# A two-layer graph convolution with experts behind it: 21 dense units ahead of the first gathered group in place of 63, kept out of the first row buffer

## The chip, the cores and the metric

The kernel runs on one core of a Trainium2 chip. The metric is the device time of one execution in microseconds (us); the time before is the median of three executions. The engines are named as the profile names them: PE (TensorE) multiplies matrices, PEld is its weight load, DVE (VectorE), ACT (ScalarE) and POOL (GpSimd) compute elementwise, POOL also issues the indirect DMAs, and SP (SyncE) issues the plain ones; SPq is its queue.

## The reference, cut to what matters

```
x: (6250, 256); src, dst, edge_weight: 100000 edges, sorted by dst
def gcn_conv(x, src, dst, w, W, b, n):
    xw = x @ W
    deg = segment_sum(w, dst)
    dinv = where(deg > 0, rsqrt(deg), 0)
    norm = dinv[src] * w * dinv[dst]
    return segment_sum(xw[src] * norm[:, None], dst) + b
out = relu(gcn_conv(layernorm(x), W1, b1))        # every node also has an edge to itself
out = gcn_conv(out, W2, b2)
x = x + relu(batchnorm(out) * gamma + beta + layernorm(x))
x = x + moe_ffn(layernorm(x))                     # 8 experts, the best two of each row, gelu
```

What the change touches is `segment_sum(xw[src] * norm)` of the first convolution: for each destination node, the weighted sum of its sources' rows. The kernel sums the rows first and multiplies by W behind that.

## The kernel before, in words

The nodes are 49 tiles of 128 (`NT`). The kernel works in three stages: it prepares the graph, it runs the two convolutions (`layer` 0 and 1 in the code; the change's words call them layer 1 and 2), and it runs batch norm, gate and experts.

**Two ways for an edge's row.** The sorted edges are 56 groups of 14 x 128. The last 40 groups (`GG`) are *gathered*: POOL issues 14 indirect DMAs a group (L575), each bringing 128 rows into the row buffer `G`; DVE builds a matrix with the edges' weights for each (`build`, L1122, into `S`); PE multiplies the two (L1554). `G` and `S` have two halves, so the gathers of group k+2 wait until the products of group k are done (`summed`). The first 16 groups are *dense*: in four blocks of four, each block a 6272 x 512 matrix of weights that POOL scatters into DRAM beforehand (L560, 224 indirect DMAs, 56 a block) and that is read back as 49 *units* of 128 x 512 (256 KB). A unit is two matmuls (L1508) against the tile's rows in `X`; 196 units make the dense part of a layer. When a block's 49 units are done, DVE adds the result to the sums (L1137) before PE goes on to the next block, and `FINISH` counts from there.

**Where the units stand.** The first `BEFORE[0]` units of layer 0 run *early*, ahead of the first gathered group: SP loads them seven at a time (`load_early`, L442) into three regions that are used in turn: `A_in` and the two halves of `G`. The others run inside the groups: `PER_GROUP` says that `up` units in `per` groups go between the 14 products. SP loads them one by one into the seven slots of `A_in` (`load_pairs`, L453), each as soon as the unit seven before it is done (`dense_used`, which PE counts up at a group's last unit). Since the early units lie in `G`, POOL's first two groups of gathers wait for `dense_used` (49 for the first, 56 for the second):

```
elif layer == 0:
    pool.wait_ge(dense_used, BEFORE[0] - (2 - k) * ASLOTS)
```

Between the early units PE also turns the 49 tiles (`turn_set`, L1498), four tiles at a time.

**The end of layer 0.** A tile is *finished* when its sums are complete: PE multiplies by W1 (`linear`, L1467), DVE adds the bias (L1059), ACT takes relu (L711), PE turns the result again (L1456) and DVE copies it (L1049); SP stores seven tiles at a time for the next layer's gathers (L466). In layer 0 a tile is finished only after the last dense unit, at most four tiles in a group, in the order of the tiles; the rest follow behind the last group (`linear_rest`, `finish_rest`). With 63 early units and five a group, the units end in group 26: groups 27 to 39 finish 46 tiles (eleven times four, then one and one, since the last tiles' edges lie in the last groups), and three are left. Layer 1's gathers (the same L575) wait for all stores.

**What sets the order.** Each engine runs its program in the order in which the code writes it; semaphores tie them together. POOL's queue in order: 224 scatters, 560 gathers of layer 0, 560 of layer 1, then its work for the experts.

Of the kernel before, what the change touches and what calls it, by code (L numbers as in the profile page):

```python
# [12 lines left out]
P = 128  # L13
CH = 7
GT = 14
# [9 lines left out]
ASLOTS = 7  # L25
# [31 lines left out]
def gnn_ffn(nc, x, src, dst, edge_weight, g_W1, g_b1, g_W2, g_b2, g_gamma, g_beta,  # L57
            gate_w, gate_b, e_W1, e_b1, e_W2, e_b2, out):
    N, D = x.shape
# [23 lines left out]
    BW = BG * P  # L83
# [15 lines left out]
    with ExitStack() as ctx:  # L99
# [17 lines left out]
        G = arena[:, 0:at]  # L117
        S = arena[:, at:at + 2 * GT * P]
# [3 lines left out]
        assert 11 * RW <= 2 * GT * P  # L122
        at += 2 * GT * P
        A_in = arena[:, at:at + ASLOTS * BW]
        early_at = [A_in] + [G[:, h * GT * D:(h + 1) * GT * D] for h in range(2)]
        assert GT * D == ASLOTS * BW
        rows_at = at + ASLOTS * BW
        src_h, dst_h, w_h, key_h = [arena[:, rows_at + n * RH:rows_at + (n + 1) * RH] for n in range(4)]
        src_h, dst_h = src_h.bitcast(I32), dst_h.bitcast(I32)
# [160 lines left out]

        LOADS = 9
        ROW_LOADS = 8
        BEFORE = (63, 0)
        assert BEFORE[0] % ASLOTS == 0 and NT % ASLOTS == 0 and (UNITS - BEFORE[0]) % ASLOTS == 0
        SETS = -(-NT // 4)
        PER_GROUP = ((5, 1), (16, 3))
        TURN_LAG = 3

        def region(q):
            return (q - BEFORE[0] // ASLOTS + 1) % 3  # L300

        def units_of(layer):
            
# [84 lines left out]
        with nc.Block() as block:  # L388
# [3 lines left out]
            def _(sp):  # L392
# [42 lines left out]
                def load_early():  # L435
                    for q in range(BEFORE[0] // ASLOTS):
                        n = q * ASLOTS
                        if n % NT == 0:
                            sp.wait_ge(paired[n // NT], 16 * BG * GT)
                        if q >= 3:  # L440
                            sp.wait_ge(dense_used, (q - 2) * ASLOTS)
                        sp.dma_start(early_at[region(q)].rearrange("p (u c) -> p u c", c=BW),  # L442
                                     pairs[n * P * BW:(n + ASLOTS) * P * BW, :].rearrange("(u p c) o -> p u (c o)", p=P, c=BW)
                                     ).then_inc(early_in[region(q)], 16)

                def load_pairs(layer):
                    for n in range(BEFORE[layer], UNITS):
# [69 lines left out]
            def _(pool):  # L517
# [46 lines left out]
                for layer in range(2):  # L564
                    for n in range(2):
                        pool.wait_ge(y_stored[n], 16 * SLOT_CH[n] * (layer + 1))
                    with pool.If(general == 0):
                        for k in range(GG):
                            if k >= 2:
                                pool.wait_ge(summed, GG * layer + k - 1)  # L570
                            elif layer == 0:
                                pool.wait_ge(dense_used, BEFORE[0] - (2 - k) * ASLOTS)
                            for j in range(GT):
                                n, t = k % 2 * GT + j, (DG + k) * GT + j
                                pool.indirect_dma_start(  # L575
                                    G[:, n * D:(n + 1) * D], None, y_tab[layer],
                                    bass.IndirectOffsetOnAxis(srcT[:, t:t + 1], 0)).then_inc(gathered[n // 2], 16)
                    with pool.Else():
                        with pool.Fori(0, ET) as i:
                            pool.wait_ge(gen_staged, i + (ET * layer + 1))  # L580
                            take_turn(gen_turn, i + (ET * layer + 1))
                            pool.indirect_dma_start(
                                G[:, 0:D], None, y_tab[layer],
                                bass.IndirectOffsetOnAxis(gstg[:, 0:1], 0)).then_inc(gen_gathered, 16)
# [258 lines left out]
            def _(dve):  # L843
# [264 lines left out]
                def aggregate(layer):  # L1108
# [9 lines left out]
                    with dve.If(general == 0):  # L1118
                        def build(k):
                            for j in range(GT):  # L1120
                                n, t = k % 2 * GT + j, (DG + k) * GT + j
                                v.tensor_scalar(S[:, n * P:(n + 1) * P], iota[:, 0:P], dst_rel[:, t:t + 1],  # L1122
                                                wT[:, t:t + 1], ALU.is_equal, ALU.mult).then_inc(s_ready, 1)

                        def base_of(k):
                            return dve.value_load(base_i[0:1, k:k + 1], min_val=0, max_val=NP - P)

                        def add_block(b):
                            for k in range(BG):
                                n = DG * layer + b * BG + k  # L1130
                                at = base_of(b * BG + k)
                                if k == 0:
                                    dve.wait_ge(dense_used, UNITS * layer + (b + 1) * NT)
                                dve.wait_ge(added, GG * layer + so_far[0])
                                dve.wait_ge(dense_added, n)
                                a = acc[:, :, bass.ds(at, P)]
                                v.tensor_tensor(a, a, psum[:, 6:8, k * P:(k + 1) * P], ALU.add).then_inc(dense_added, 1)  # L1137
                            so_far[1] += BG

                        def add_group(k):  # L1140
                            at = base_of(DG + k)
                            dve.wait_ge(sum_turned, GG * layer + k + 1)
                            dve.wait_ge(added, GG * layer + k)
                            dve.wait_ge(dense_added, DG * layer + so_far[1])
                            a = acc[:, :, bass.ds(at, P)]
                            v.tensor_tensor(a, a, bank(2 * (k % 2) + 1, D).rearrange("p (c n) -> p c n", c=KC),  # L1146
                                            ALU.add).then_inc(added, 1)
                            so_far[0] += 1

                        so_far = [0, 0]  # L1150
                        blocks = 0
                        build(0)
                        for k, (first_unit, units) in enumerate(units_of(layer)):
                            while blocks < NB and (blocks + 1) * NT <= first_unit:
                                add_block(blocks)
                                blocks += 1
                            if k + 1 < GG:
                                build(k + 1)
                            while blocks < NB and (blocks + 1) * NT <= first_unit + units:
                                add_block(blocks)  # L1160
                                blocks += 1
                            if layer == 1 and k and 0 in FINISH[1][1][k - 1]:
                                set_shift(chain_fast)
                            for i in FINISH[layer][1][k]:
                                finish(layer, i)
                            add_group(k)
                        dve.wait_ge(added, GG * (layer + 1))
                        v.memset(dscr[:, :], 0.0).then_inc(agg_done, 1)
                        finish_rest(layer, NT - len(FINISH[layer][2]), chain_fast)
# [213 lines left out]
            def _(pe):  # L1383
# [104 lines left out]
                def aggregate(layer):  # L1488
# [13 lines left out]
                    with pe.If(general == 0):  # L1502
                        def unit(n, table):
                            b, t = divmod(n, NT)
                            if t == 0 and b + NB * layer:
                                pe.wait_ge(dense_added, BG * (NB * layer + b))
                            for c in range(KC):
                                ins = m.matmul(bank(6 + c, BW), X[:, t * D + c * P:t * D + (c + 1) * P], table,  # L1508
                                               start=(t == 0), stop=(t == NT - 1))
                            return ins  # L1510
# [19 lines left out]
                        if layer == 0:  # L1530
                            for n in range(3):
                                turn_set(n)
                            sets, batches = 3, BEFORE[0] // ASLOTS
                            for q in range(batches):
                                pe.wait_ge(early_in[region(q)], q // 3 * 16 + 16)
                                for u in range(ASLOTS):
                                    ins = unit(q * ASLOTS + u, early_at[region(q)][:, u * BW:(u + 1) * BW])
                                    if u == ASLOTS - 1:
                                        ins.then_inc(dense_used, ASLOTS)
                                    if u % 3 == 2 and sets < SETS:  # L1540
                                        turn_set(sets)
                                        sets += 1
                        pe.wait_ge(self_added, NT * (layer + 1))
                        used = 0
                        for k, (first_unit, units) in enumerate(units_of(layer)):
# [190 lines left out]
```

## Time and profile before

| | |
|---|---|
| time, median of 3 runs | 2427.9 us (2425.14 to 2429.19) |
| profiled execution: span from its first to its last instruction | 2758.3 us |
| busy in it: PE / POOL / DVE / ACT | 2008.3 / 1699.3 / 899.0 / 424.7 us |
| mean granted TensorE clock | 0.826 |

The profiled execution is 330.4 us longer than the median of the timed ones; its rows have to be read with that in mind. In a row of the timeline stand the start, the duration, the engine, the line, the operation, the tiles, how often, and in brackets the idle time before it and what ended that. An fp32 matmul is two rows of PE, so a dense unit is four rows and a group's 14 products are 28.

### The profile page before, as it was taken

The numbers are of one execution on the slowest core, as the hardware profiler recorded it, in microseconds if no ns is written. First come the engines' busy times: TensorE is split into PE (matmuls) and PEld (weight loads), VectorE is DVE, ScalarE is ACT, GpSimd is POOL, SyncE is SP. The second block draws the span as 40 slices with busy tenths as digits, with TensorE's granted clock in tenths as the row PEclk, the third lists the DMA queues.
The fourth block names the chain that finished last, engine by engine and source line by source line (L and its number), as shares of the span: only waits on it lengthen the run. The fifth ranks groups of instructions, "written<-read, shape, count | busy, mean of one in ns | idle before, by whom it ended". The sixth has DMA issues, their size and how long they took to land.

```text
span 2758.3 us, 29927 instructions
## 1 busy us (share of the span) xinstructions
PE 2008.3 (73%) x8514; PEld 1397.0 (51%) x8515; DVE 899.0 (33%) x2676; ACT 424.7 (15%) x1140; POOL 1699.3 (62%) x1679
## 2 busy tenths in 40 slices
PE   0353249887778886665688888888885473999998
PEld 0251014444445444554445555554554362899997
DVE  7970001111122113342113323232323776333332
ACT  1610000000000000111000000000000465344443
POOL 2887732566656666665765666755665544566665
PEclk6555559988889987878889999998998555999999
DMA  9993013454445443334444545544545313688885
GB/s 321 336 312 101 27 40 124 135 165 152 147 138 168 147 151 103 119 117 119 142 148 143 175 154 170 158 145 141 170 154 186 101 58 129 179 209 207 214 210 137
DMA packets 263529, 431.17 MB, mean 156 GB/s; under 512 B 38800, under 2 KB 147023, under 8 KB 263279
## 3 DMA queue, kind: packets, MB, share of 16 engines
q1 hardware_dynamic: 180591, 253.79, 27.8%
q0 software_dynamic: 81088, 173.80, 23.8%
q10 hardware_dynamic: 1728, 2.13, 0.2%
q8 instruction: 55, 0.90, 0.1%
q14 instruction: 67, 0.55, 0.1%
HBM read 339.36 MB, written 91.16 MB: 156 GB/s over the span
## 4 chain that ended last, share of the span: by engine, by line
another core or an unknown queue 34%; PE 28%; issue 17%; DVE 13%; DMA 3%; ACT 1%; SPq 1%; POOL 1%; DVEq 1%; POOLq 0%; ACTq 0%
PE psum L1508 8%; PE psum L1679 6%; PE psum L1687 6%; PE psum L1554 4%; DVE arena L1122 3%; DMA arena<-pair_weights 1%; DMA out_dram<-ACC 1%; PE psum L1467 1%; SPq L453 1%; PE psum L1670 1%; DVE edge_cols L1214 1%; DVE stats L1220 1%; PE psum L1526 1%; DVE ACC L926 1%
## 5 line engine op out<-in xcount | busy, mean ns | idle before, releaser
L575 POOL DMA_INDIRECT arena<-conv_rows,edge_cols x1120 | 1065.3, 951 | 694.3 <-issue 338.7
L1508 PE MATMUL psum<-arena,X 128*128 128x512 f32 x1568 | 805.7, 636 | 220.5 <-issue 141.4
L1554 PE MATMUL psum<-arena 128*128 128x256 f32 x2240 | 595.3, 399 | 78.2 <-issue 64.8
L1554 PEld LDWEIGHTS psum<-arena 128*128 128x128 f32 x2240 | 447.1, 203 | 271.1 <-issue 218.1
L1508 PEld LDWEIGHTS psum<-arena,X 128*128 128x128 f32 x1568 | 314.6, 202 | 512.8 <-issue 434.4
L1146 DVE TENSOR_TENSOR ACC<-ACC,psum 128x256 f32 x80 | 33.8, 422 | 1037.9 <-remote 441.5
L560 POOL DMA_INDIRECT pair_weights<-scale_b,mean_b x224 | 252.3, 1126 | 116.7 <-issue 67.9
L1122 DVE TENSOR_SCALAR arena<-iota,edge_cols 128x128 f32<-128x128 f32 x1120 | 298.1, 359 | 6.1 <-issue 5.9
L650 POOL DMA_INDIRECT out_dram<-ACC x105 | 166.3, 1583 | 108.9 <-DMA out_dram<-ACC 78.3
L729 ACT ACTIVATE arena<-psum 128x256 f32<-128x256 f32 x80 | 30.4, 380 | 1311.7 <-remote 727.5
L1679 PE MATMUL psum<-ACC,arena 128*128 128x128 f32 x1680 | 208.3, 277 | 0.2 <-DVE ACC L1356 0.2
L1679 PEld LDWEIGHTS psum<-ACC,arena 128*128 128x128 f32 x1680 | 199.4, 194 | 0.6 <-issue 0.6
L1687 PE MATMUL psum<-arena,ACC 128*128 x840 | 198.9, 380 | 0.2 <-ACT ACC L820 0.2
L1687 PEld LDWEIGHTS psum<-arena,ACC 128*128 128x128 f32 x840 | 151.7, 191 | 16.9 <-issue 0.6
L1526 PE MATMUL psum<-ident,arena 128*128 128x128 f32 x160 | 38.3, 326 | 155.2 <-ACT arena L729 143.1
L820 ACT ACTIVATE ACC<-psum,b1e 128x128 f32<-128x128 f32 x420 | 120.1, 369 | 108.7 <-issue 69.0
L1374 DVE TENSOR_TENSOR ACC<-psum,b2e 128x256 f32<-128x256 f32 x105 | 44.7, 425 | 252.1 <-PE psum L1687 178.1
L638 POOL DMA_INDIRECT ACC<-rows_for_experts,ACC x105 | 103.4, 985 | 35.7 <-issue 25.3
L1526 PEld LDWEIGHTS psum<-ident,arena 128*128 128x128 f32 x160 | 20.5, 156 | 203.6 <-ACT arena L729 174.9
L1114 DVE COPY ACC<-psum 128x512 f32<-128x512 f32 (+1 forms) x25 | 15.9, 675 | 227.6 <-remote 179.8
L1427 PE MATMUL psum<-ACC,arena 128*128 128x6 bf16 x784 | 56.2, 202 | 34.9 <-DVE arena L993 30.4
L721 ACT ACTIVATE ln<-ACC 128x256 f32<-128x256 f32 x49 | 20.4, 417 | 359.7 <-issue 173.9
(287 smaller groups left out, 1532.4 us busy)
## 6 DMA issues: line engine op xcount, KB each, us to landing
arena<-pair_weights SPq DMA_DIRECT2D x329, 256.0 KB
arena<-in_L_ffn_W_dram SPq DMA_DIRECT2D x113, 512.0 KB, 7.9
pair_weights<-zeros SPq DMA_DIRECT2D x4, 12544.0 KB, 44.2
arena<-conv_rows,edge_cols POOLq DMA_INDIRECT x1120
arena<-pair_weights SPq DMA_DIRECT2D x9, 1792.0 KB
conv_rows<-X SPq DMA_DIRECT2D x14, 896.0 KB
X<-in_x_dram SPq DMA_DIRECT2D x12, 896.0 KB
rows_for_experts<-ACC SPq DMA_DIRECT2D x7, 910.0 KB, 4.2
```

The source lines that it names most:

```text
L560: pool.indirect_dma_start(pairs, bass.IndirectOffsetOnAxis(cell_i[:, t:t + 1], 0), cell_w[:, t:t + 1], None).then_inc(paired[b], 16)
L575: pool.indirect_dma_start(G[:, n * D:(n + 1) * D], None, y_tab[layer], bass.IndirectOffsetOnAxis(srcT[:, t:t + 1], 0)).then_inc(gathered[n ...
L638: pool.indirect_dma_start(xs[:, u * DX:(u + 1) * DX], None, rows_x, bass.IndirectOffsetOnAxis(slot_i[:, n:n + 1], 0)).then_inc(xs_in[u // ...
L650: pool.indirect_dma_start(out, bass.IndirectOffsetOnAxis(slot_i[:, n:n + 1], 0), ys[:, u * D:(u + 1) * D], None, bounds_check=N - 1, oob_i ...
L820: ins = a.activation(hT[:, slot * H + c * P:slot * H + (c + 1) * P], psum[:, 2 + slot, c * P:(c + 1) * P], ACT.Gelu, bias=b1e[:, bass.ds(e ...
L1122: v.tensor_scalar(S[:, n * P:(n + 1) * P], iota[:, 0:P], dst_rel[:, t:t + 1], wT[:, t:t + 1], ALU.is_equal, ALU.mult).then_inc(s_ready, 1)
L1427: ins = m.matmul(bank(2 + h, 6 * DQ)[:, r * 6:(r + 1) * 6], hot[:, :, j], w_group[:, (q * GT + j) * 6:(q * GT + j + 1) * 6], start=(j == 0 ...
L1508: ins = m.matmul(bank(6 + c, BW), X[:, t * D + c * P:t * D + (c + 1) * P], table, start=(t == 0), stop=(t == NT - 1))
L1526: ins = m.transpose(bank(2 * (k % 2) + 1, D)[:, c * P:(c + 1) * P], sum_rows[:, at:at + P], ident[:, :])
L1554: ins = m.matmul(bank(2 * (k % 2), D), S[:, n * P:(n + 1) * P], G[:, n * D:(n + 1) * D], start=(j == 0), stop=(j == GT - 1))
L1679: ins = m.matmul(psum[:, 2 + s, c * P:(c + 1) * P], w1s[:, s4 * KC * H + k * H + c * P:s4 * KC * H + k * H + (c + 1) * P], xsT[:, s * D + ...
L1687: ins = m.matmul(bank(4 + s, D), hT[:, s * H + c * P:s * H + (c + 1) * P], w2e[:, bass.ds(e * (HC * D) + c * D, D)], start=(c == 0), stop= ...
```

## The change

It takes 21 early units in place of 63. They are three loads, each with a region of its own: the second half of `G`, `A_in`, and the buffer `S` of DVE's matrices. So the first half of `G` is free from the start: the first group of gathers waits for no unit, the second for seven. DVE builds its first matrices only after all 21 are done, since `S` holds units until then. The other 175 units of layer 0 go six to a group. PE turns a set of tiles after every second early unit, not every third, and the sets that are left behind the last.

```
-        early_at = [A_in] + [G[:, h * GT * D:(h + 1) * GT * D] for h in range(2)]
-        assert GT * D == ASLOTS * BW
+        early_at = [G[:, GT * D:2 * GT * D], A_in, S]
+        assert GT * D == ASLOTS * BW == 2 * GT * P
...
-        BEFORE = (63, 0)
+        BEFORE = (21, 0)
...
-        PER_GROUP = ((5, 1), (16, 3))
+        PER_GROUP = ((6, 1), (16, 3))
...
-        def region(q):
-            return (q - BEFORE[0] // ASLOTS + 1) % 3
+        assert BEFORE[0] == len(early_at) * ASLOTS
...
                     for q in range(BEFORE[0] // ASLOTS):
...
-                        if q >= 3:
-                            sp.wait_ge(dense_used, (q - 2) * ASLOTS)
-                        sp.dma_start(early_at[region(q)].rearrange("p (u c) -> p u c", c=BW),
+                        sp.dma_start(early_at[q].rearrange("p (u c) -> p u c", c=BW),
...
                             if k >= 2:
                                 pool.wait_ge(summed, GG * layer + k - 1)
-                            elif layer == 0:
-                                pool.wait_ge(dense_used, BEFORE[0] - (2 - k) * ASLOTS)
+                            elif layer == 0 and k == 1:
+                                pool.wait_ge(dense_used, ASLOTS)
...
+                        if layer == 0:
+                            dve.wait_ge(dense_used, BEFORE[0])
                         build(0)
...
-                                    if u % 3 == 2 and sets < SETS:
+                                    if u % 2 == 1 and sets < SETS:
                                         turn_set(sets)
                                         sets += 1
+                            for n in range(sets, SETS):
+                                turn_set(n)
```

On POOL, where the gathers of layer 0 begin, the rows stood so before (a name in brackets is the semaphore that the row waits for):

```order
43 L567 COMPARE_AND_BRANCH [waits y_stored0,y_stored1,sc_set,src_ready]
44 L575 DMA arena<-conv_rows,edge_cols 128x256 [waits dense_used]
45 L575 DMA arena<-conv_rows,edge_cols 128x256 x13
46 L575 DMA arena<-conv_rows,edge_cols 128x256 [waits dense_used]
47 L575 DMA arena<-conv_rows,edge_cols 128x256 x13
48 L575 DMA arena<-conv_rows,edge_cols 128x256 [waits summed]
```

The same place of the change, where lines are up to three lower in number:

```order
43 L564 COMPARE_AND_BRANCH [waits y_stored0,y_stored1,sc_set,src_ready]
44 L572 DMA arena<-conv_rows,edge_cols 128x256 x14
45 L572 DMA arena<-conv_rows,edge_cols 128x256 [waits dense_used]
46 L572 DMA arena<-conv_rows,edge_cols 128x256 x13
47 L572 DMA arena<-conv_rows,edge_cols 128x256 [waits summed]
```

The first 14 gathers have lost their wait for `dense_used`; those of the second group keep it, for the value 7 in place of 56.

On DVE, behind the last group of layer 0 (L1168 marks the end of the sums), three tiles were left to finish before, L1059 and a copy each:

```order
683 L1146 TENSOR_TENSOR ACC<-ACC,psum 128x2x128
684 L1168 MEMSET dscr 128x1
685 L1059 SCALAR_TENSOR_TENSOR tmp<-psum,dinv,b1g 128x256
686 L1049 COPY ACC<-psum 128x2x128
687 L1059 SCALAR_TENSOR_TENSOR tmp<-psum,dinv,b1g 128x256
688 L1049 COPY ACC<-psum 128x2x128
689 L1059 SCALAR_TENSOR_TENSOR tmp<-psum,dinv,b1g 128x256
690 L1049 COPY ACC<-psum 128x2x128 x4
```

The change at the same place (L1167 is the mark; of nine pairs the first three and the last stand here):

```order
670 L1143 TENSOR_TENSOR ACC<-ACC,psum 128x2x128
671 L1167 MEMSET dscr 128x1
672 L1056 SCALAR_TENSOR_TENSOR tmp<-psum,dinv,b1g 128x256
673 L1046 COPY ACC<-psum 128x2x128
674 L1056 SCALAR_TENSOR_TENSOR tmp<-psum,dinv,b1g 128x256
675 L1046 COPY ACC<-psum 128x2x128
676 L1056 SCALAR_TENSOR_TENSOR tmp<-psum,dinv,b1g 128x256
...
688 L1056 SCALAR_TENSOR_TENSOR tmp<-psum,dinv,b1g 128x256
689 L1046 COPY ACC<-psum 128x2x128 x4
```

Nine tiles are left in place of three: the units now end in group 29, so ten groups of four finish 40 of the 49.

## Rows read from the trace of the kernel before

**Rows 1.** The page: span, costliest group (busy, mean ns, idle and its releaser)

```profile
span 2758.3 us, 29927 instructions
...
L575 POOL DMA_INDIRECT arena<-conv_rows,edge_cols x1120 | 1065.3, 951 | 694.3 <-issue 338.7
```

**Rows 2.** Timeline of POOL, 376 to 518 us: last scatter, first gathers of three groups

```profile
377.01 0.96 POOL L560 DMA_INDIRECT pair_weights<-scale_b,mean_b  x1 [0.31 <-issue]
460.80 0.98 POOL L575 DMA_INDIRECT arena<-conv_rows,edge_cols  x1 [82.82 <-PE psum L1508]
...
477.14 0.95 POOL L575 DMA_INDIRECT arena<-conv_rows,edge_cols  x1 [0.30 <-issue]
479.30 0.95 POOL L575 DMA_INDIRECT arena<-conv_rows,edge_cols  x1 [1.21 <-PE psum L1508]
...
517.20 0.94 POOL L575 DMA_INDIRECT arena<-conv_rows,edge_cols  x1 [20.66 <-PE psum L1554]
```

**Rows 3.** Timeline of PE over the early units and the first group

```profile
221.06 6.83 PE L1508 MATMUL psum<-arena,X 128*128 128x512 f32 x12 [33.51 <-DMA arena<-pair_weights]
227.73 1.04 PE L1498 MATMUL psum<-ident,X 128*128 128x128 f32 x8
...
240.01 1.01 PE L1508 MATMUL psum<-arena,X 128*128 128x512 f32 x1 [2.53 <-issue]
242.81 1.01 PE L1508 MATMUL psum<-arena,X 128*128 128x512 f32 x1 [1.79 <-issue]
...
434.61 25.91 PE L1508 MATMUL psum<-arena,X 128*128 128x512 f32 x60
463.71 27.25 PE L1508 MATMUL psum<-arena,X 128*128 128x512 f32 x56 [3.19 <-DVE ACC L1137]
...
502.92 3.78 PE L1508 MATMUL psum<-arena,X 128*128 128x512 f32 x4 [10.67 <-DMA arena<-pair_weights]
```

**Rows 4.** Busy time by stretch, 235 to 396 and 396 to 461 us

```profile
core 0: us, PE busy (x) PEld busy (x) DVE busy (x) ACT busy (x) POOL busy (x), PEclk, DMA share, GB/s
...
235.00:396.00 161.00, 46.88 (x58) 14.51 (x57) 3.87 (x6) 0.00 (x0) 108.56 (x114) 0.51 0.05 12
396.00:461.00 65.00, 63.71 (x174) 30.45 (x174) 12.18 (x28) 0.00 (x0) 0.20 (x1) 0.96 0.41 141
```

**Rows 5.** The gathers' line: durations, first and last start

```profile
L575 POOL DMA_INDIRECT arena<-conv_rows,edge_cols x1120: 943/949/1142, 460.8 to 2136.6; - x187
```

**Rows 6.** Timeline of POOL: three groups' first gathers, last gather of layer 0

```profile
1092.66 0.94 POOL L575 DMA_INDIRECT arena<-conv_rows,edge_cols  x1 [2.91 <-remote]
...
1112.83 0.94 POOL L575 DMA_INDIRECT arena<-conv_rows,edge_cols  x1 [2.94 <-remote]
...
1290.29 0.95 POOL L575 DMA_INDIRECT arena<-conv_rows,edge_cols  x1 [0.30 <-issue]
1308.76 0.95 POOL L575 DMA_INDIRECT arena<-conv_rows,edge_cols  x1 [17.52 <-issue]
```

**Rows 7.** Timeline of PE inside a group: six rows of products, then a unit

```profile
511.18 1.88 PE L1508 MATMUL psum<-arena,X 128*128 128x512 f32 x4
512.89 1.46 PE L1554 MATMUL psum<-arena 128*128 128x256 f32 x6
514.19 1.88 PE L1508 MATMUL psum<-arena,X 128*128 128x512 f32 x4
```

**Rows 8.** SP's line for the units inside the groups: first and last issue

```profile
L453 SPq DMA_DIRECT2D arena<-pair_weights x329: 162/430/1638, 500.2 to 2072.9; - x165
```

**Rows 9.** Timeline of all engines behind the last group of layer 0

```profile
1298.51 0.48 DVE L1059 SCALAR_TENSOR_TENSOR tmp<-psum,dinv,b1g 128x256 f32<-128x256 f32 x1 [1.10 <-PE psum L1467]
...
1299.60 0.48 DVE L1059 SCALAR_TENSOR_TENSOR tmp<-psum,dinv,b1g 128x256 f32<-128x256 f32 x1 [0.27 <-PE psum L1467]
...
1300.68 0.48 DVE L1059 SCALAR_TENSOR_TENSOR tmp<-psum,dinv,b1g 128x256 f32<-128x256 f32 x1 [0.27 <-PE psum L1467]
...
1301.73 0.36 SPq L466 DMA_DIRECT2D conv_rows<-X  x1
```

More of the change, by code:

```diff
@@ L439, in load_early @@
                             sp.wait_ge(paired[n // NT], 16 * BG * GT)
-                        if q >= 3:
-                            sp.wait_ge(dense_used, (q - 2) * ASLOTS)
-                        sp.dma_start(early_at[region(q)].rearrange("p (u c) -> p u c", c=BW),
+                        sp.dma_start(early_at[q].rearrange("p (u c) -> p u c", c=BW),
                                      pairs[n * P * BW:(n + ASLOTS) * P * BW, :].rearrange("(u p c) o -> p u (c o)", p=P, c=BW)
-                                     ).then_inc(early_in[region(q)], 16)
+                                     ).then_inc(early_in[q], 16)
                 def load_pairs(layer):
@@ L1534, in aggregate @@
                             for q in range(batches):
-                                pe.wait_ge(early_in[region(q)], q // 3 * 16 + 16)
+                                pe.wait_ge(early_in[q], 16)
                                 for u in range(ASLOTS):
-                                    ins = unit(q * ASLOTS + u, early_at[region(q)][:, u * BW:(u + 1) * BW])
+                                    ins = unit(q * ASLOTS + u, early_at[q][:, u * BW:(u + 1) * BW])
                                     if u == ASLOTS - 1:
                                         ins.then_inc(dense_used, ASLOTS)
-                                    if u % 3 == 2 and sets < SETS:
+                                    if u % 2 == 1 and sets < SETS:
                                         turn_set(sets)
                                         sets += 1
+                            for n in range(sets, SETS):
+                                turn_set(n)
                         pe.wait_ge(self_added, NT * (layer + 1))
```

## The prediction

> **What bounds the kernel now.** I read the page first: the costliest group is POOL's gathers, and the engine stands still before them for 694.3 us in all [rows 1]. Then POOL's timeline from its last scatter on. That scatter ends at 377.01 + 0.96 = 378.0 us; POOL then idles 82.8 us, until PE has done 49 early units, and starts the first gather at 460.80; the third group waits another 20.7 us, for the products of the first [rows 2]. This is the wait that the change attacks, so the question is where it comes from, and whether the timed executions have it at all.
>
> PE's timeline shows where it comes from in the profiled one. PE starts on the units at 221.06; undisturbed rows follow each other at 25.91 / 60 = 0.43 us, so a unit of four rows is 1.72 us [rows 3]. But between 240 and 396 us single rows stand 2.80 us apart, with nothing that ends the idle time but "issue" [rows 3]; in the 161 us from 235 to 396 PE got through 58 rows, at a granted clock of 0.51 (the lower of its two levels, 1.2 GHz), and a DMA share of 0.05 [rows 4]. The clock does not explain that: at this level a row of a unit takes 1.01 us [rows 3], and 2.80 us pass. From 396 us on, PE runs at 0.96 of the clock again and packs 174 rows into 65 us [rows 4]. So in the profiled execution PE lost some 140 us in a stretch in which it waited for no semaphore that the profile shows.
>
> Is that stretch in the timed executions? The span is 2758.3 us [rows 1], the median 2427.9 us: 330.4 us less. I made a sum of what the execution would take if nothing but POOL's own issue set its pace from the scatters to the last gather. The scatters end, with the usual gap of 0.30 us, at 378.3. A group of 14 gathers goes from 460.80 to 477.14 + 0.95 + 0.30 = 478.39: 17.6 us [rows 2]; 40 groups are 703.6 us. Between the layers lie 17.2 us more (1308.76 less 1290.29 + 0.95 + 0.30) [rows 6]. Layer 1's 40 groups are again 703.6. From the last gather (2136.6 + 1.25) [rows 5] to the end of the span are 620.4 us. The sum is 378.3 + 703.6 + 17.2 + 703.6 + 620.4 = 2423 us, 4.8 us below the median. With the 82.5 us of waiting in it the sum is 2506, and with the trace's own pace of the groups, 1112.83 - 1092.66 = 20.2 us even where no unit stands between the products [rows 6], it is more again. The median has room for neither. I take it that the timed executions are paced by POOL's issue and that PE's slow stretch belongs to the profiled one. This is an inference from a sum, not a row, and the first rival is its denial.
>
> **A rule that says otherwise.** The Trainium skill ("Runtime: NRT & Kernel Launch", section "The launch sequence") says that a profile's total is longer than the reported execution by a gap of about 6.2 us, whatever the kernel. By that rule the timed executions would be an estimated 2752 us with every wait of the profile in them, and rival 1 would be the forecast; the median of 2427.9 us does not agree, and the measurement decides.
>
> **The change part by part, in a timed execution so paced.**
>
> *The first gather.* At 0.43 us a row PE would do the 49 units by 221.1 + 196 x 0.43 + ten sets of turned tiles at 228.60 - 227.73 = 0.87 us [rows 3] = 314 us, and all 63 by 345, with the 3.2 us for which PE waits for DVE's block [rows 3]. The scatters end at 378.3 either way, and the gathers stand behind them in POOL's queue. So the old wait is over 60 us before POOL comes to it: taking it away is worth nothing. What hides it is POOL's own 224 scatters; if that cover were gone, the trace's 82.5 us would be the price. The six loads fewer on SP (1.8 MB each) lie under the scatters too, and DVE's new wait ahead of its first matrices ends with the 21st unit, before 270 us at this pace, with nothing behind it in DVE's queue that is needed before the first product at about 380.
>
> *Six units a group.* PE's work for a group is 28 rows of products at 1.30 / 6 us = 6.1 us and five units at 1.71 us [rows 7] = 14.6 us; with six it is 16.3. POOL needs 17.6 for a group, so PE still keeps up, with 1.3 us to spare in place of 3.0. Four blocks now end inside the groups (4, 12, 20, 29) and not three; each holds PE up by some 3.2 us [rows 3], which the spare time wins back over three groups, and PE may fall behind by most of a group before gathers wait for it. The loads: with seven slots and six units a group, one unit is loaded ahead and the next is asked for when the group before it ends. SP's first issue at 500.2 [rows 8] let PE go on at 502.92 [rows 3]: 2.7 us. The second unit of a group is needed after five products and one unit, 5 x 0.43 + 1.71 = 3.9 us. It fits by 1.2 us. Bounds for this part: 0, and all 42 moved units on the path, 42 x 1.71 = 72 us. I take 0, since both margins, thin as they are, come from rows.
>
> *The end of layer 0.* Nine tiles are left behind the last group in place of three. There the engines have nothing else, and a tile follows the other at (1300.68 - 1298.51) / 2 = 1.09 us, DVE waiting for PE's matmul each time; right behind the last one stands SP's store, for which layer 1's first gather waits [rows 6, 9]. Six tiles more are 6.5 us on the path. Nothing hides them: POOL's queue is empty there. The tiles that moved out of groups 27 to 29 leave PE time that nobody needs. Bounds: 0, if the store or the clock swallows it, and 6 x 2.2 = 13 us, if PE should run there at its lower level.
>
> Sum: 0 + 0 + 6.5. Against the profiled execution's own time the first part would count in full: 2758.3 - 82.5 + 6.5 = 2682 us for its span, if the slow stretch falls as before. For the timed median I carry the difference over: 2427.9 + 6.5 = **2434 us**. A measurement of this kernel can tell a change of about 0.2%, 4.9 us, from none; the forecast lies just outside.
>
> **The rivals.**
>
> 1. *The wait is real.* PE's slow stretch is in the timed executions as well, and something else makes up the 330 us. For it: the rows [rows 2, 3], which are all that was recorded. Against it: the sum above; with the first gather at 460.8, the median leaves (2427.9 - 460.8 - 17.2 - 620.4) / 80 = 16.6 us a group, less than POOL's 17.6. Then the first gather moves by 82.5 us and the third group by up to 517.2 - (378.3 + 2 x 17.6) = 104 us, and 6.5 come back: 2331 to 2352 us; I take 2352. This is the other side of the forecast.
> 2. *PE becomes the bound in layer 0.* 16.3 us of 17.6 leave 1.3 us; whatever holds PE up for longer in each group, a load that lands later than 2.7 us above all, is added some 29 times. At 2 us a group it is 29 x (16.3 + 2 - 17.6) = 20 us on top of the 6.5: 2454 us; at the upper bound 2506. It decides from 1.3 us a group on. For it: PE already does 14.6 of 17.6 us and the trace has PE late in many groups (10.67 us for one load at 502.92 [rows 3]). Against it: that load was late because SP could issue it only at 500.2 [rows 8]; with 21 early units the first seven loads are asked for over 100 us ahead.
> 3. *Nothing measurable.* The six tiles are partly hidden, or the start gives back a few us because the timed PE is not quite at full pace there: 2428 us.
>
> **How the numbers follow.** The forecast of a small loss at the layer's end has 0.50, rival 1 has 0.15, rival 2 has 0.15, rival 3 has 0.20. The likeliest one's own range is 2428 to 2441 (the bounds of the six tiles: 0 and 13 us, the second at twice 1.09 us a tile). The range reaches to rival 2 above, and below far enough to hold a start that gives back up to a third of the 82.5 us: 2400 to 2462; rival 1 and the far end of rival 2 lie outside, under 0.2 together. Slower by more than 0.2%: 0.35 of the forecast's 0.50 and rival 2, 0.50. Within: 0.15 of the forecast and 0.15 of rival 3, 0.30. Faster: rival 1 and the rest, 0.20.
>
> **What the changed kernel's profile would show.** The first gather right behind the last scatter, near 378 us, in place of 460.80: that would show the edit does what it says, and by itself it says nothing on the timed median. A span shorter by far more than the median is: that would bear out that the wait belonged to the profiled execution. Nine rows of DVE's bias behind the last group, about 1.09 us apart, and 23 to 24 us between the last gather of layer 0 and the first of layer 1, not 17.5. Groups with six units whose gathers still start 17.5 to 20.2 us apart; 21 or more would be rival 2. The forecast is wrong if the median falls by tens of us, and then the step that failed is the sum that put the slow stretch outside the timed executions.

## The result and the profile after

The change takes 2430.64 us (median of 18 executions, 2426.18 to 2432.78), the kernel before 2426.27 us beside it (18 executions, 2420.67 to 2429.19): a ratio of 1.0017 [1.0011, 1.0023], 4.4 us slower. That is inside the 0.2% that the prediction took for no change; the interval shows that it is a loss all the same, and of the forecast sign: 2434 and +6.5 us were predicted.

The page of the change, span and gathers:

```profile
span 2431.0 us, 29957 instructions
...
L572 POOL DMA_INDIRECT arena<-conv_rows,edge_cols x1120 | 1066.9, 953 | 366.1 <-issue 366.1
```

Against [rows 1] the profiled execution is 327 us shorter (2758.3 to 2431.0) where the timed ones became 4.4 us longer. A reader of the two profiles alone would report 12% of gain. POOL's idle time before the gathers fell from 694.3 to 366.1 us, and none of it is now put down to PE.

Timeline of POOL, last scatter and first gather:

```profile
377.32 0.96 POOL L557 DMA_INDIRECT pair_weights<-scale_b,mean_b  x1 [0.30 <-issue]
378.58 0.98 POOL L572 DMA_INDIRECT arena<-conv_rows,edge_cols  x1 [0.31 <-issue]
```

The gather stands right behind the scatter, at 378.58 in place of 460.80 [rows 2]. From here to the end of the layer POOL issues without a stop.

Timeline of PE with six units a group: the wait at a block's end, and the first products of two groups, six groups apart:

```profile
475.28 2.44 PE L1507 MATMUL psum<-arena,X 128*128 128x512 f32 x4 [2.31 <-DVE ACC L1134]
...
497.91 1.46 PE L1555 MATMUL psum<-arena 128*128 128x256 f32 x6
...
597.29 1.46 PE L1555 MATMUL psum<-arena 128*128 128x256 f32 x6
```

Behind the block's end PE is late and runs without a wait for six groups: (597.29 - 497.91) / 6 = 16.56 us a group, against POOL's 17.6. It makes up a microsecond a group and POOL never comes to wait for it.

Timeline of all engines at the end of layer 0: last gather, last products, the bias rows of the tiles left, first gather of layer 1:

```profile
1080.78 0.95 POOL L572 DMA_INDIRECT arena<-conv_rows,edge_cols  x1 [0.31 <-issue]
...
1085.03 1.10 PE L1555 MATMUL psum<-arena 128*128 128x256 f32 x4 [1.11 <-DMA arena<-conv_rows,edge_cols]
...
1089.77 0.48 DVE L1056 SCALAR_TENSOR_TENSOR tmp<-psum,dinv,b1g 128x256 f32<-128x256 f32 x1 [2.04 <-PE psum L1466]
...
1091.55 0.48 DVE L1056 SCALAR_TENSOR_TENSOR tmp<-psum,dinv,b1g 128x256 f32<-128x256 f32 x1 [0.93 <-PE psum L1466]
...
1092.63 0.48 DVE L1056 SCALAR_TENSOR_TENSOR tmp<-psum,dinv,b1g 128x256 f32<-128x256 f32 x1 [0.27 <-PE psum L1466]
...
1099.14 0.48 DVE L1056 SCALAR_TENSOR_TENSOR tmp<-psum,dinv,b1g 128x256 f32<-128x256 f32 x1 [0.27 <-PE psum L1466]
...
1106.75 0.94 POOL L572 DMA_INDIRECT arena<-conv_rows,edge_cols  x1 [25.02 <-issue]
```

Nine bias rows stand from 1089.77 to 1099.14. From the third on they follow each other at 1.08 us, and POOL is idle for 25.0 us between the layers. The profile says "issue" for that idle time; what POOL waits for there is the store behind the ninth tile: the view of the store's line (L463) names POOL's 25.0 us as the wait for it.

### The profile page after: what moved, and what is told of

The parts are those of the page before. It is cut to its first block, busy times and chain, and to the rows that moved or that the text cites. A ratio compares the mean times of both kernels' runs of the same rounds, so it can differ in the third digit from the quotient of the medians.

```text
span 2431.0 us, 29957 instructions
## 1 busy us (share of the span) xinstructions
PE 1910.6 (79%) x8514; PEld 1353.7 (56%) x8515; DVE 898.5 (37%) x2676; ACT 426.4 (18%) x1140; POOL 1699.6 (70%) x1679
## 4 chain that ended last, share of the span: by engine, by line
POOL 55%; issue 18%; PE 16%; DVE 6%; DMA 3%; ACT 1%; SPq 0%; POOLq 0%; DVEq 0%; ACTq 0%
POOL arena L572 44%; POOL pair_weights L557 10%; PE psum L1680 7%; PE psum L1688 7%; DMA out_dram<-ACC 1%; PE psum L1671 1%; DVE edge_cols L1213 1%; DVE stats L1219 1%; DVE X L1216 1%; PE psum L1466 1%; DMA rows_for_experts<-ACC 1%; PE psum L1629 0%; DVE ACC L1322 0%; DVE ACC L1208 0%; DMA arena<-conv_rows,edge_cols 0%
## 5 line engine op out<-in xcount | busy, mean ns | idle before, releaser
L572 POOL DMA_INDIRECT arena<-conv_rows,edge_cols x1120 | 1066.9, 953 | 366.1 <-issue 366.1
L1507 PE MATMUL psum<-arena,X 128*128 128x512 f32 x1568 | 745.9, 600 | 46.8 <-DMA arena<-pair_weights 32.8
L1555 PEld LDWEIGHTS psum<-arena 128*128 128x128 f32 x2240 | 423.5, 196 | 460.0 <-issue 363.8
L1507 PEld LDWEIGHTS psum<-arena,X 128*128 128x128 f32 x1568 | 299.7, 192 | 264.9 <-issue 212.3
L1688 PEld LDWEIGHTS psum<-arena,ACC 128*128 128x128 f32 x840 | 151.5, 190 | 17.2 <-issue 0.9
L718 ACT ACTIVATE ln<-ACC 128x256 f32<-128x256 f32 x49 | 20.4, 417 | 355.0 <-DVE ACC L1063 344.3
L1426 PEld LDWEIGHTS psum<-ACC,arena 128*128 128x128 bf16 x784 | 51.5, 158 | 39.6 <-DVE arena L990 39.6
L831 ACT ACTIVATE ACC<-ACC,wcol 128x256 f32<-128x256 f32 x105 | 53.5, 510 | 113.2 <-DVE ACC L1373 113.2
L593 POOL TENSOR_TENSOR edge_cols<-edge_cols,bet 128x256 f32<-128x256 f32 x49 | 44.7, 945 | 31.7 <-DVE bet L1199 26.3
```

The costliest lines, as they stand in the source:

```text
L572: pool.indirect_dma_start(G[:, n * D:(n + 1) * D], None, y_tab[layer], bass.IndirectOffsetOnAxis(srcT[:, t:t + 1], 0)).then_inc(gathered[n ...
L831: a.activation(ys[:, y * D:(y + 1) * D], yb[:, (u % 2) * D:(u % 2 + 1) * D], ACT.Copy, scale=wcol[:, y:y + 1]).then_inc(ys_ready, 1)
L1426: ins = m.matmul(bank(2 + h, 6 * DQ)[:, r * 6:(r + 1) * 6], hot[:, :, j], w_group[:, (q * GT + j) * 6:(q * GT + j + 1) * 6], start=(j == 0 ...
L1555: ins = m.matmul(bank(2 * (k % 2), D), S[:, n * P:(n + 1) * P], G[:, n * D:(n + 1) * D], start=(j == 0), stop=(j == GT - 1))
L1688: ins = m.matmul(bank(4 + s, D), hT[:, s * H + c * P:s * H + (c + 1) * P], w2e[:, bass.ds(e * (HC * D) + c * D, D)], start=(c == 0), stop= ...
```

## The experiments

The change has three parts: the start, six units a group, nine tiles left. The first four runs take them apart, two more vary the dose, and the rest ask where the 2 us between forecast and result went.

### The kernel before, profiled once more

No edit. This tells whether the 82.8 us of waiting in [rows 2] is the kernel's or that one execution's.

> The kernel before, unchanged, profiled once more. Theory (the slow stretch of PE between 235 and 396 us belonged to that one profiled execution; timed executions are paced by POOL's issue): ratio 1.000; the new profile has its first gather of layer 0 near 378 us, no idle time of POOL put down to PE at the first three groups, a span within 5 us of the median 2426 (not 2758), and about 18 to 20 us between the last gather of layer 0 and the first of layer 1. Rival (the wait is part of every execution): first gather again near 460 us.

Ratio 0.9997 [0.9988, 1.0006]. The new profile has a span of 2422.6 us. Its stretches from the windows (busy time of PE, PEld, DVE, ACT, POOL, then granted clock, DMA share, GB/s):

```profile
235.00:346.00 111.00, 107.81 (x295) 50.90 (x293) 19.81 (x49) 0.00 (x0) 84.35 (x88) 0.97 0.33 100
```

PE's timeline, the last two stretches of early units, the second up to the 63rd:

```profile
290.23 25.91 PE L1508 MATMUL psum<-arena,X 128*128 128x512 f32 x60
319.33 27.25 PE L1508 MATMUL psum<-arena,X 128*128 128x512 f32 x56 [3.19 <-DVE ACC L1137]
```

And POOL's and DVE's rows at the first gather and between the layers, with the last products of PE:

```profile
379.13 0.98 POOL L575 DMA_INDIRECT arena<-conv_rows,edge_cols  x1 [0.30 <-issue]
...
1079.56 0.95 POOL L575 DMA_INDIRECT arena<-conv_rows,edge_cols  x1 [0.30 <-issue]
...
1083.76 2.04 PE L1554 MATMUL psum<-arena 128*128 128x256 f32 x4 [1.23 <-DMA arena<-conv_rows,edge_cols]
...
1089.69 0.48 DVE L1059 SCALAR_TENSOR_TENSOR tmp<-psum,dinv,b1g 128x256 f32<-128x256 f32 x1 [2.04 <-PE psum L1467]
...
1091.82 0.48 DVE L1059 SCALAR_TENSOR_TENSOR tmp<-psum,dinv,b1g 128x256 f32<-128x256 f32 x1 [1.28 <-PE psum L1467]
...
1093.73 0.48 DVE L1059 SCALAR_TENSOR_TENSOR tmp<-psum,dinv,b1g 128x256 f32<-128x256 f32 x1 [1.05 <-PE psum L1467]
...
1101.24 0.94 POOL L575 DMA_INDIRECT arena<-conv_rows,edge_cols  x1 [20.73 <-issue]
```

The same program, and where [rows 4] had 58 rows in 161 us there are 295 in 111 us, at a clock of 0.97. The 49th unit is done at 290.23 + 25.91 = 316.1 us and the 63rd at 346.6; the first gather starts at 379.13 without a wait. The slow stretch of [rows 3] was of one execution. It is not all that was slow there: some 82 of the 330 us lie ahead of the first gather, and nearly all the others in the two layers, where a group of gathers took 20.7 us on average ((1290.29 + 1.25 - 460.80) / 40 in layer 0, [rows 2, 6]) and takes 17.5 here. What made that execution slow, no run here shows. The idle time between the layers is 20.7 us here, not the 17.5 of [rows 6]; that matters below.

### Before, waiting for all 63 units

```
-                                pool.wait_ge(dense_used, BEFORE[0] - (2 - k) * ASLOTS)
+                                pool.wait_ge(dense_used, BEFORE[0])
```

> Before, with the first two groups of gathers waiting for all 63 early units in place of 49 and 56. Theory (PE is through the 63 units by about 345 us, before POOL comes to its first gather at 378): ratio 1.000, first gather at about 378 us. Rival (the wait is real in timed executions): 14 units at 1.72 us or more are added, 24 us and up, ratio 1.010 or more.

Ratio 1.0000 [0.9991, 1.0009]. PE's last early units and POOL's first gather:

```profile
318.47 27.14 PE L1508 MATMUL psum<-arena,X 128*128 128x512 f32 x56 [3.19 <-DVE ACC L1137]
```

```profile
379.04 0.98 POOL L575 DMA_INDIRECT arena<-conv_rows,edge_cols  x1 [0.30 <-issue]
```

Even a wait for all the units is over 33 us before POOL arrives. So there was nothing at the start for the change to win.

### Before, with nine tiles left

```
-                while n < NT and len(mine) < most and free[order[n]] <= k:
+                while n < (40 if layer == 0 else NT) and len(mine) < most and free[order[n]] <= k:
```

> Before, with 63 early units and five a group as they were, but layer 0 finishes at most 40 tiles inside its groups, so that nine are left behind the last group in place of three. Theory (the whole loss is six more tiles at the layer's end): 4.4 to 6.5 us slower than before, ratio 1.0018 to 1.0027, as much as the change itself. Rival (the loss comes from six units a group or from the start): ratio 1.000.

Ratio 1.0029 [1.0017, 1.0040], 6.4 us by the medians: the loss appears without any other part of the change. The idle time between the layers is 26.1 us, 5.4 more than before:

```profile
1107.15 0.94 POOL L575 DMA_INDIRECT arena<-conv_rows,edge_cols  x1 [26.10 <-issue]
```

### The change, with three tiles left

Six tiles a group in place of four, at products 2, 4, 6 and so on:

```
-                most = 1 if layer == 1 and n == 0 else 2 if k in ends else 4 - layer
+                most = 1 if layer == 1 and n == 0 else 2 if k in ends else (6, 3)[layer]
...
-                                if j % 3 == 2 and j // 3 < len(FINISH[layer][1][k]):
-                                    i = FINISH[layer][1][k][j // 3]
+                                at, step = (j // 2 - 1, j >= 2 and j % 2 == 0) if layer == 0 else (j // 3, j % 3 == 2)
+                                if step and at < len(FINISH[layer][1][k]):
+                                    i = FINISH[layer][1][k][at]
```

> The change, with up to six tiles finished in a group of layer 0 in place of four (ten groups, so three are left behind the last as in before). Theory (the loss is the six tiles): it gives back 4.4 to 6.5 us against the change, ratio to before 1.000, and the gap between the last gather of layer 0 and the first of layer 1 shrinks from 25.0 to about 18.5 us. Rival (six units a group, or the start): stays at 1.0017.

Ratio 1.0002 [0.9993, 1.0011]: the loss is given back. The idle time is 20.4 us, that of the kernel before and not the 18.5 expected:

```profile
1100.19 0.94 POOL L572 DMA_INDIRECT arena<-conv_rows,edge_cols  x1 [20.45 <-issue]
```

21 early units and six a group are still in this kernel. Together they cost nothing that 0.1% would show. With the run before, the tiles left at the layer's end are the whole loss.

### The change, with five units a group

`PER_GROUP = ((5, 1), (16, 3))`: the units end in group 34, and 29 tiles are left.

> The change with five units a group in place of six: 21 early units, the units end in group 34 and 29 tiles are left behind the last group in place of nine. Theory (tiles left cost 1.09 us each): 20 x 1.09 = 22 us slower than the change, about 2448 to 2453 us, ratio to before 1.010 to 1.012. Rival (the change's loss comes from six units a group): no slower than before.

2448.05 us, ratio 1.0101 [1.0086, 1.0117], 25.3 us above before beside it (2422.73) and so 21 above the change. First and last bias row behind the last group, and the first gather of layer 1:

```profile
1088.17 0.48 DVE L1056 SCALAR_TENSOR_TENSOR tmp<-psum,dinv,b1g 128x256 f32<-128x256 f32 x1 [1.10 <-PE psum L1466]
...
1118.53 0.48 DVE L1056 SCALAR_TENSOR_TENSOR tmp<-psum,dinv,b1g 128x256 f32<-128x256 f32 x1 [0.27 <-PE psum L1466]
```

```profile
1126.24 0.94 POOL L572 DMA_INDIRECT arena<-conv_rows,edge_cols  x1 [45.24 <-issue]
```

29 rows, (1118.53 - 1088.17) / 28 = 1.084 us apart. Twenty tiles more idle POOL for 45.24 - 25.02 = 20.2 us more. The price per tile holds over a threefold dose.

### The change, with seven units a group

`PER_GROUP = ((7, 1), (16, 3))`: the units end in group 24, and three tiles are left.

> The change with seven units a group: the units end in group 24, three tiles are left, as in before. Theory (PE becomes the bound past POOL's 17.6 us; six units took 16.55 us a group where PE was behind, a seventh 1.71 more, 18.3): 25 groups x 0.7 us and four block ends of 3.2 us, less some 13 us of slack, 17 us or more slower than the change without its six tiles, and up to 75 us if each group waits for its loads too, since none is loaded ahead: ratio 1.007 to 1.03, with POOL waiting for PE. Rival (PE has room to spare): the six tiles come back, ratio 1.000.

2491.16 us, ratio 1.0272 [1.0255, 1.0288]: here PE is the bound, as rival 2 had it. POOL's waits (total, times, longest), and PE's first unit of a group:

```profile
POOL arena L572 <- PE psum L1555: 74.6, 21, 5.1
```

```profile
575.51 1.99 PE L1507 MATMUL psum<-arena,X 128*128 128x512 f32 x4 [1.92 <-DMA arena<-pair_weights]
```

Two groups' first gathers start 20.5 us apart:

```profile
571.29 0.94 POOL L572 DMA_INDIRECT arena<-conv_rows,edge_cols  x1 [3.64 <-PE psum L1555]
...
591.75 0.94 POOL L572 DMA_INDIRECT arena<-conv_rows,edge_cols  x1 [3.08 <-PE psum L1555]
```

So the gathers run at PE's pace, POOL waits for PE 21 times, and in each group PE waits about 2 us for a load, since seven slots for seven units leave none to load ahead. The margin of the six-unit plan is real, and one unit wide.

### Where the 2 us between forecast and result went: later tiles

In the kernel before, the last group has one tile to finish. This edit leaves 46 tiles inside the groups, but none in group 27, two in 28 and four in each of 29 to 39:

```
-                most = 1 if layer == 1 and n == 0 else 2 if k in ends else 4 - layer
+                most = 1 if layer == 1 and n == 0 else 2 if k in ends or (layer, k) == (0, 28) else 0 if layer == 0 and k < 28 else 4 - layer
```

> Before, with the same 46 tiles finished inside the groups, but later: none in group 27, two in 28, four in each of 29 to 39, three left as before. Theory (the 2.1 us that the change's loss stays below the forecast are PE's clock: in the last group of before PE has one tile to finish and takes 2.04 us for the last products, 2.1 and 1.9 us for the first tiles; with four tiles in the last group it is at the upper level there): the gap between the last gather of layer 0 and the first of layer 1 shrinks from 20.7 by 1.5 to 2.5 us, the last products take 1.10 us, ratio 0.999. Rival (the clock has nothing to do with the tiles in the last group): gap 20.7 us, ratio 1.000.

2418.88 us, ratio 0.9987 [0.9978, 0.9996]: faster than both kernels. Last products, first and last bias row, first gather:

```profile
1083.17 1.10 PE L1554 MATMUL psum<-arena 128*128 128x256 f32 x4 [0.75 <-DMA arena<-conv_rows,edge_cols]
...
1086.96 0.48 DVE L1059 SCALAR_TENSOR_TENSOR tmp<-psum,dinv,b1g 128x256 f32<-128x256 f32 x1 [1.10 <-PE psum L1467]
...
1089.13 0.48 DVE L1059 SCALAR_TENSOR_TENSOR tmp<-psum,dinv,b1g 128x256 f32<-128x256 f32 x1 [0.27 <-PE psum L1467]
...
1096.56 0.94 POOL L575 DMA_INDIRECT arena<-conv_rows,edge_cols  x1 [16.38 <-issue]
```

The idle time fell by 4.3 us, twice what was expected. The windows from 1080 to 1090 us, whose last three numbers are the granted clock, the DMA share and GB/s. Before, profiled again:

```profile
1080.00:1090.00 10.00, 7.20 (x17) 4.59 (x18) 0.79 (x3) 0.38 (x1) 0.51 (x1) 0.50 0.15 26
```

Before with nine tiles left:

```profile
1080.00:1090.00 10.00, 6.78 (x15) 4.16 (x16) 0.48 (x2) 0.38 (x1) 0.95 (x1) 0.50 0.20 30
```

The change:

```profile
1080.00:1090.00 10.00, 6.84 (x28) 4.84 (x27) 2.34 (x7) 1.40 (x3) 1.43 (x2) 0.88 0.20 37
```

Before with later tiles:

```profile
1080.00:1090.00 10.00, 7.46 (x36) 5.64 (x36) 3.80 (x11) 2.33 (x6) 0.18 (x1) 1.00 0.13 22
```

The change with three tiles left, which has one tile in its last group:

```profile
1080.00:1090.00 10.00, 6.60 (x18) 4.33 (x18) 1.33 (x4) 0.78 (x2) 0.00 (x0) 0.58 0.13 17
```

With one tile in the last group (before) or none (before with nine left) PE ends the layer at 0.50 of its clock, the 1.2 GHz level; with four tiles it is at 1.00, and in the change, which also has four there, at 0.88. The change with three tiles left, at 0.58, has the low clock and the idle time (20.4 us) of the kernel before. PE is about equally busy in all five (6.6 to 7.5 of 10 us), but gets through 28 and 36 rows in place of 15 to 18. The first tile behind the last group shows where the change stands between the two; PE's products with W1, before (profiled again), in the change and with later tiles:

```profile
1087.58 2.08 PE L1467 MATMUL psum<-W1g,ACC 128*128 128x256 f32 x4 [0.61 <-DVE ACC L1146]
```

```profile
1087.66 2.07 PE L1466 MATMUL psum<-W1g,ACC 128*128 128x256 f32 x4 [0.61 <-DVE ACC L1143]
```

```profile
1085.79 1.13 PE L1467 MATMUL psum<-W1g,ACC 128*128 128x256 f32 x4 [0.61 <-DVE ACC L1146]
```

The change does its last products at the upper level (1.10 us, against 2.04 before), but its clock has fallen by the first tile left; with later tiles it does not fall. The Trainium skill ("TensorE: Matmul & The Clock Gate", section "Part 1: The HAM clock gate") says that the clock follows how busy PE has been of late. The trace agrees in the work done: from 1066 to 1080 us PE got through 31 and 26 rows in before and in before with nine left, and through 41 and 44 in the change and with later tiles. By busy time it does not sort them: 8.7 and 9.6 us against 9.1 and 10.7.

### A split last store, and loads held back

On top of the later tiles, the last store of seven tiles is split into four and three (the counts that wait for it follow):

```
-                    sp.wait_ge(y_ready, CH * (c + 1))
-                    sp.dma_start(rows_of(y_tab[1], c), tile3(X[:, c * CH * D:(c + 1) * CH * D])).then_inc(y_stored[c % 2], 16)
+                    for first, last in ((0, CH),) if c < NCH - 1 else ((0, 4), (4, CH)):
+                        t0, t1 = c * CH + first, c * CH + last
+                        sp.wait_ge(y_ready, t1)
+                        sp.dma_start(y_tab[1][bass.ds(t0 * P, (t1 - t0) * P), :].rearrange("(t p) d -> p t d", p=P),
+                                     tile3(X[:, t0 * D:t1 * D], t1 - t0)).then_inc(y_stored[c % 2], 16)
```

> The kernel with late tiles, and the last store of seven tiles split: four tiles as soon as they are finished, three behind the last. Theory (the store's 5.4 us to landing are partly its 896 KB): 512 KB less on the path at some 370 GB/s, 1.4 us off the gap between the layers on top of the late tiles, ratio 0.998 to 0.999. Rival (the 5.4 us are latency): no further change, ratio that of the kernel with late tiles.

2418.64 us, ratio 0.9982 [0.9973, 0.9991]. The DMA issues (KB each, us to landing) and the first gather:

```profile
conv_rows<-X SPq DMA_DIRECT2D x1, 512.0 KB, 2.9
conv_rows<-X SPq DMA_DIRECT2D x1, 384.0 KB, 4.2
```

```profile
1095.21 0.94 POOL L578 DMA_INDIRECT arena<-conv_rows,edge_cols  x1 [15.45 <-issue]
```

The idle time fell by 0.9 us. The timed runs cannot tell that from none; the traces do: a second profile of this kernel, below, has 15.49 us, and two profiles with the end of the kernel before (profiled again, and waiting for all units) lie 0.3 us apart, at 20.7 and 20.4. The 384 KB take longer to land than the 512 KB, and right behind them seven unit loads are issued; so the next kernel lets SP wait for the stores before these loads, and the one with the split store ran again beside it:

```
+                for n in range(2):
+                    sp.wait_ge(y_stored[n], 32 * SLOT_CH[n] + 16 * (1 - n))
                 with sp.If(general == 0):
                     load_pairs(1)
```

> The kernel with late tiles and the split store, and SP issues layer 1's first seven unit loads only when the stores have landed. Theory (the last store's 384 KB take 4.2 us to landing, longer than the 512 KB ahead of it with 2.9 us, because seven loads of 256 KB are issued right behind it and share the DMA engines): the last store lands in 2.5 to 3 us, the gap between the layers falls from 15.5 to about 14 us, ratio to before 0.997 to 0.998; the loads come some 3 us later, before the first products need them. Rival (the store's landing does not depend on what is issued behind it): gap 15.5 us, no change, or a loss where PE waits for the first units.

> The kernel with late tiles and the split store once more, beside the one with the loads held back, on the same chip. Every theory: ratio 0.998, gap 15.5 us; it says how far two measurements of one kernel lie apart here.

Held back: 2418.96 us, ratio 0.9985 [0.9977, 0.9994]. Split again: 2419.11 us, ratio 0.9983 [0.9975, 0.9992]. The store with nothing behind it:

```profile
conv_rows<-X SPq DMA_DIRECT2D x1, 384.0 KB, 4.3
```

```profile
1096.30 0.94 POOL L580 DMA_INDIRECT arena<-conv_rows,edge_cols  x1 [15.61 <-issue]
```

4.3 us with the loads held back, 4.2 with them: the theory fell, the loads do not slow the store. Why 384 KB take longer here than 512 KB some 6 us earlier stays open.

## Why the prediction was right

**The sum that puts the slow stretch outside the timed executions** held. It gave the 49th unit at 314 us, the 63rd at 345 and the first gather at 378.3; the second profile of the kernel before has 316.1, 346.6 and 379.13. A group takes POOL 17.5 us there ((1101.24 - 20.73 - 379.13) / 40), against 17.6. The term between the layers was too small: 17.2 where 20.4 are measured (20.7 less the usual gap of 0.3), since it was read in the disturbed execution. The total came out well in part because its errors cancel: layer 0's groups were 1.9 us too long in it (703.6 against 701.7) and the stretch behind the last gather 2.8 (620.4 against 2422.6 - 1803.8 - 1.25 = 617.6, from the second profile). The rule weighed against the sum, in the Trainium skill ("Runtime: NRT & Kernel Launch", section "The launch sequence"), speaks of a profile's total; the prediction put the span, from the first to the last instruction, in its place, so no run here tests the 6.2 us. For the span the record is clear: in the eleven executions that were both profiled and timed the time is 1.8 to 1.9 us longer than the span (2432.78 against 2431.0 for the change), and no fixed gap accounts for the 330 us of the first profile.

**The first gather, worth nothing**: right. It moved by 82 us in the profiles and by 0.55 us against an undisturbed profile (379.13 to 378.58), and a longer wait in before costs nothing either. Rival 1, a median of 2352 us, is out.

**Six units a group, at nothing**: right, in both its parts. PE's 16.3 us a group measured 16.56, POOL never waits, and the change with three tiles left is level with before. Rival 2 did not come at six units; at seven it came with 68 us.

**Six tiles at the layer's end, 6.5 us**: the mechanism is right (nine left in before loses as much, three left in the change gives it back), the size was off by 2 us. The term took 1.09 us for every tile, and that is what each further tile costs. But it compared with three tiles that it supposed at the same pace, as [rows 9] show them. There PE came late to the layer's end and did 22 rows of products without a stop right before:

```profile
1289.52 6.29 PE L1554 MATMUL psum<-arena 128*128 128x256 f32 x22
```

In an undisturbed execution of before the three tiles are dearer. From the end of the last gather to the first bias row it takes 1089.69 - 1080.51 = 9.2 us (1079.56 + 0.95 is that end) and 8.0 in the change; the bias rows span 4.0 us and 9.4; from the last one to the next gather it is 7.5 and 7.6. The sum is 20.7 and 25.0, a difference of 4.3, as the medians have it. The change lost 5.3 us on tiles and won 1.1 us ahead of them, because with four tiles in its last group PE does the last products at the upper level of its clock; the forecast did not consider what the last group leaves PE to do. The run with later tiles gives before the same four tiles there and gains 4 us by it. The idle time was forecast at 23 to 24 us and is 25.0: its base was taken 3.2 us too small and its growth 2.2 us too large.

**Rival 3**, nothing measurable, is close to the truth in size (4.4 us are less than 0.2%) but wrong in its reason: nothing was given back at the start, and all six tiles lie on the path. So the likeliest outcome of the prediction, slower by more than 0.2% (0.50), did not come; a change within 0.2% had 0.30.

## What to carry to other kernels

Before costing the wait that a profile shows, add up what the execution would take without it and compare with the timed median: a span 330 us above the median says that some of its waits are not there when it counts. Work that is moved out of a stage's cover lands at the stage's end, at the full price of a chain in which nothing else runs. And the last steps of a stage can be cheaper if PE has work right up to them: here, moving covered work later, not earlier, gained 4 us where this change lost 4.

## What the runs showed of the hardware

One execution of an unchanged program had PE issue single matmuls mostly 2.80 us apart for some 150 us, at a granted clock of 0.51 and with no wait in the profile [rows 3, 4]; in the 40 us from 225 us on PE got through 44 rows there, and through 128 to 148 in each of the other eleven profiles. PE's granted clock at the end of a layer depended on whether the last group still had tiles to finish: 0.50 to 0.58 with none or one, 0.88 to 1.00 with four; in the run with later tiles that was worth 4.3 us of a gap of 20.7. A store of 384 KB took 4.2 to 4.3 us to land, one of 512 KB ahead of it 2.9, in each of three profiles.
